# A Mamba-2 and FFN layer on one core: the Newton steps of the row factor and the sum of squares over column tiles move from VectorE to GpSimd

## The reference

```python
xn = _layernorm(x)
x = x + (xn + _mamba2(xn, w_in, conv_w, conv_b, dt_bias, A_log, D, norm_w, w_out)) + _ffn(xn, W1, W2, W3)
# _mamba2, with 16 heads of 64 (1024 inner columns) and a state of 128:
zxbcdt = xn @ w_in
xBC = silu(causal_conv4(zxbcdt[xBC columns]) + conv_b)
y = _ssd(xh * dt, dt * A, Bm, Cm) + xh * D
y = y * silu(z)
y = y * rsqrt(mean(y * y, axis=-1) + EPS) * norm_w      # the part that the change touches
return y @ w_out
# _ffn: silu(xn @ W1.T) * (xn @ W3.T), a Walsh-Hadamard transform over 2048 columns, @ W2.T
```

## Time and profile before

| | |
|---|---|
| median of 3 runs | 1002.5 us (1000.33 to 1004.55) |
| the profiled execution's own time | 1000.4 us |
| its span | 998.6 us |
| TensorE busy | 939.4 us (94%) |
| VectorE busy | 615.0 us (62%) |
| ScalarE busy | 352.1 us (35%) |
| GpSimd busy | 296.0 us (30%) |
| mean granted clock of TensorE | 0.982 |
| chain that ended last | TensorE 77%, VectorE 9%, issue 4%, ScalarE 4%, DMA 3%, GpSimd 3% |

### The profile page before, as it was taken

One profiled execution on the slowest core, in us unless ns is written; L12 is line 12 of the kernel. 1 busy time (PEld: TensorE's weight loads), 2 busy tenths in 40 slices (PEclk: granted clock), 3 DMA queues, 4 the chain that ended last, 5 costly groups with the idle time before them and its releaser, 6 DMA issues.

```text
span 998.6 us, 13195 instructions
## 1 busy us (share of the span) xinstructions
PE 939.4 (94%) x4960; PEld 469.5 (47%) x4960; DVE 615.0 (62%) x1063; ACT 352.1 (35%) x537; POOL 296.0 (30%) x180
## 2 busy tenths in 40 slices
PE   3797868999799999999999999999999999999997
PEld 2343333555344444555545445554545445555543
DVE  5776477779543576747762576766651766776721
ACT  5574744443423333331221343332221344232200
POOL 0332241636000021655500102654400202665300
PEclk9899997999899999999999999999999999999999
DMA  9589553746332433554421433554322535265122
GB/s 323 222 301 342 169 180 112 226 140 220 111 121 95 161 101 109 181 138 112 120 85 64 161 106 129 146 151 132 108 65 64 176 102 154 78 149 148 43 76 94
DMA packets 80815, 142.64 MB, mean 143 GB/s; under 512 B 8048, under 2 KB 20976, under 8 KB 78704
## 3 DMA queue, kind: packets, MB, share of 16 engines
q1 hardware_dynamic: 61536, 113.79, 35.7%
q10 hardware_dynamic: 19216, 28.01, 9.6%
HBM read 115.82 MB, written 25.95 MB: 142 GB/s over the span
## 4 chain that ended last, share of the span: by engine, by line
PE 77%; DVE 9%; issue 4%; ACT 4%; DMA 3%; POOL 3%; ACTq 0%; SPq 0%; DVEq 0%; POOLq 0%
PE ps L569 50%; PE ps L774 16%; PE ps L739 2%; PE ps L731 2%; DMA arena<-cs_rows 1%; DVE arena L1113 1%; PE ps L725 1%; PE ps L694 1%; DVE arena L1162 1%; PE ps L711 1%; ACT arena L862 1%; ACT arena L835 1%; POOL arena L1355 1%; DVE arena L1183 1%; POOL arena L1343 1%
## 5 line engine op out<-in xcount | busy, mean ns | idle before, releaser
L569 PE MATMUL ps<-xh,arena 128*128 128x512 f16 x1600 | 499.7, 386 | 28.4 <-DVE arena L1178 8.7
L569 PE MATMUL ps<-xl,arena 128*128 128x512 f16 x800 | 308.4, 385 | 0.0
L569 PEld LDWEIGHTS ps<-xh,arena 128*128 128x128 f16 x1600 | 160.4, 100 | 223.5 <-DVE arena L1113 25.8
L774 PE MATMUL ps<-arena 128*128 128x512 f16 x768 | 171.2, 379 | 0.0
L1328 POOL TENSOR_TENSOR arena<-arena 128x512 f16<-128x512 f32 x64 | 81.7, 1281 | 277.8 <-ACT arena L914 277.8
L1343 POOL TENSOR_TENSOR arena<-arena 128x2048 f32<-128x2048 f32 x16 | 57.8, 3612 | 286.6 <-DMA arena<-cs_rows 286.6
L569 PEld LDWEIGHTS ps<-xl,arena 128*128 128x128 f16 x800 | 79.2, 99 | 91.3 <-issue 7.3
L1162 DVE SCALAR_TENSOR_TENSOR arena<-ps,cw,arena 128x511 f32<-128x511 f32 (+2 forms) x120 | 89.5, 748 | 47.1 <-ACT arena L904 45.2
L774 PEld LDWEIGHTS ps<-arena 128*128 128x128 f16 x768 | 74.5, 98 | 91.2 <-issue 5.7
L914 ACT ACTIVATE arena<-arena 128x512 f16<-128x512 f32 x64 | 40.3, 630 | 207.6 <-DVE arena L1183 207.6
L569 PE MATMUL ps<-wo_hi,arena 128*128 128x512 f16 x256 | 78.8, 379 | 0.6 <-DVE arena L1291 0.6
(11 more groups left out here) (158 smaller groups left out, 1070.6 us busy)
## 6 DMA issues: line engine op xcount, KB each, us to landing
arena<-w_parts SPq DMA_DIRECT2D x198, 256.0 KB, 2.7
w_parts<-arena SPq DMA_DIRECT2D x66, 256.0 KB, 3.1
arena<-cs_rows ACTq DMA_DIRECT2D x16, 1024.0 KB, 6.0
arena<-w SPq DMA_DIRECT2D x8, 1024.0 KB, 8.6
arena<-w SPq DMA_DIRECT2D x32, 256.0 KB, 4.1
arena<-ecs_rows ACTq DMA_DIRECT2D x24, 256.0 KB, 7.9
arena<-w SPq DMA_DIRECT2D x8, 512.0 KB, 6.5
w_mid<-arena SPq DMA_DIRECT2D x16, 256.0 KB, 2.8
```

The lines of the kernel that those rows point to most:

```text
L569: ins = nc.tensor.matmul(out_ap, lhs(i, a), rhs(i, c), start=(i == 0 and s == 0), stop=(i == n - 1 and s == 2))
L774: ins = nc.tensor.matmul(bank(t), hw[a][:, i, t * P:(t + 1) * P], w2s[i % W2R][:, d, :], start=(i == 0 and s == 0), stop=(i == JF - 1 and ...
```

## The change

- The sum over column tiles (Q) is GpSimd's: three additions in place on `t1` (512, 256 and 128 columns wide, the last one into sqr), each waiting for the one before it.
- The three Newton steps are GpSimd's, as a new step ROW of 12 instructions of 128x1, which stands one FFN tile behind V. VectorE still makes the seed, and a column nmh = -0.5 * nv.
- The row factor moves from V to W on VectorE, and waits there for the root.
- V waits on TensorE also for yscl_ok; VectorE's t1 product waits for the sum of the chunk before.
- Four semaphores of the weight norms become one that counts to four (not shown: only names and numbers of the waits differ).

```diff
 STEP_FIRST = {"T": (3, 8, 17, 26), "E": (None, 7, 14, 22), "X": (4, 11, 18, 29), "Y": (7, 14, 22, 32), "N": (9, 16, 24, 34), "Q": (9, 16, 24, 34),
-              "V": (11, 18, 26, 36), "W": (14, 20, 28, 38)}
+              "V": (11, 18, 26, 36), "ROW": (12, 19, 27, 37), "W": (14, 20, 28, 38)}
 PREP_FIRST = {"LN": 28}
...
     "V": (10, 18, 26, 36),
+    "ROW": (11, 19, 27, 37),
     "W": (12, 20, 28, 38),
...
         Bs, Gm = view(P), view(P)
-        sqr, small = view(P), view(8)
-        ssum, ytot, yhalf, yscl, yinv, nv, nr, ntmp = (small[:, i:i + 1] for i in range(8))
+        sqr, small = view(P), view(9)
+        ssum, ytot, yhalf, yscl, yinv, nv, nr, ntmp, nmh = (small[:, i:i + 1] for i in range(9))
         row = view(1)
...
         mamba_evac = signal("mamba_evac", NC, 1)
+        guess_ok = signal("guess_ok", NC)
+        root_ok = signal("root_ok", NC)
         ln_ok = signal("ln_ok", 1)
...
                     elif kind == "V":
+                        pe.wait_ge(yscl_ok.sem, yscl_ok.at(b, c))
                         pe.wait_ge(sqr_ok.sem, sqr_ok.at(b, c))
...
                             dve.wait_ge(d_ecsb, (b * (NC - 1) + c) * 32)
+                            dve.wait_ge(sqr_ok.sem, sqr_ok.at(b, c - 1))
                             nc.vector.tensor_tensor(t1, bank(6, 2), ecsb, ALU.mult).then_inc(t1_ok.sem, 1)
...
                                                        op0=ALU.mult, op1=ALU.mult).then_inc(ygate_ok.sem, 1)
-                    elif kind == "Q":
-                        dve.wait_ge(sq_ok.sem, sq_ok.at(b, c))
-                        nc.vector.tensor_reduce(out=sqr, in_=t1.rearrange("p (q l) -> p l q", q=QE), axis=AX.X,
-                                                op=ALU.add).then_inc(sqr_ok.sem, 1)
                     elif kind == "N":
...
                         dve.wait_ge(mean_read.sem, mean_read.at(b, c))
-                        rsqrt(dve, steps, nv, nr, ntmp, yhalf)
-                        k = steps.step(nc.vector.tensor_scalar(row, nr, yinv, f_out[:, 0:1], ALU.mult, ALU.mult))
+                        k = steps.step(nc.vector.tensor_scalar(ntmp.bitcast(I32), nv.bitcast(I32), 1, None, ALU.logical_shift_right))
+                        steps.step(nc.vector.tensor_scalar(nmh, nv, -0.5, None, ALU.mult))
+                        dve.wait_ge(steps.sem, k)
+                        nc.vector.tensor_scalar(nr.bitcast(I32), ntmp.bitcast(I32), -1, 0x5F3759DF, ALU.mult,
+                                                ALU.add).then_inc(guess_ok.sem, 1)
                     elif kind == "W":
...
                                                                ALU.mult, ALU.add))
+                        dve.wait_ge(root_ok.sem, root_ok.at(b, c))
+                        k = steps.step(nc.vector.tensor_scalar(row, nr, yinv, f_out[:, 0:1], ALU.mult, ALU.mult))
                         dve.wait_ge(steps.sem, k)
...
         def _(pool):
+            newton = Steps(pool_steps)
             for b in range(NB):
...
                                                     ALU.mult).then_inc(xdec_ok.sem, 1)
+                    elif kind == "Q":
+                        pool.wait_ge(sq_ok.sem, sq_ok.at(b, c))
+                        k = newton.step(nc.gpsimd.tensor_tensor(t1[:, 0:4 * P], t1[:, 0:4 * P], t1[:, 4 * P:8 * P], ALU.add))
+                        pool.wait_ge(newton.sem, k)
+                        k = newton.step(nc.gpsimd.tensor_tensor(t1[:, 0:2 * P], t1[:, 0:2 * P], t1[:, 2 * P:4 * P], ALU.add))
+                        pool.wait_ge(newton.sem, k)
+                        nc.gpsimd.tensor_tensor(sqr, t1[:, 0:P], t1[:, P:2 * P], ALU.add).then_inc(sqr_ok.sem, 1)
+                    elif kind == "ROW":
+                        pool.wait_ge(guess_ok.sem, guess_ok.at(b, c))
+                        for n in range(3):
+                            k = newton.step(nc.gpsimd.tensor_tensor(ntmp, nr, nr, ALU.mult))
+                            pool.wait_ge(newton.sem, k)
+                            k = newton.step(nc.gpsimd.tensor_tensor(ntmp, ntmp, nmh, ALU.mult))
+                            pool.wait_ge(newton.sem, k)
+                            k = newton.step(nc.gpsimd.tensor_scalar(ntmp, ntmp, 1.5, None, ALU.add))
+                            pool.wait_ge(newton.sem, k)
+                            ins = nc.gpsimd.tensor_tensor(nr, ntmp, nr, ALU.mult)
+                            if n < 2:
+                                k = newton.step(ins)
+                                pool.wait_ge(newton.sem, k)
+                        ins.then_inc(root_ok.sem, 1)
                     elif kind == "S" and c > 0:
...
```

More of the change, by code:

```diff
@@ L234, in build @@
             sb(n, [P, 1]) for n in ("f_in", "f_half0", "f_half", "f_13", "f_out", "f_w2", "f_had"))
-        arena_words = 45669
+        arena_words = 45670
         arena = sb("arena", [P, arena_words])
@@ L344, in build @@
         guards = sem("guards")
-        sum_g0, sum_g1, sum_w2, sum_wo = sem("sum_g0"), sem("sum_g1"), sem("sum_w2"), sem("sum_wo")
+        norm_sums = sem("norm_sums")
         scale_g0, scale_g1, scale_13, scale_w2, scale_wo = (
@@ L418, in build @@
         ecst_ok = signal("ecst_ok", 1)
-        dve_steps, act_steps = sem("dve_steps"), sem("act_steps")
+        dve_steps, act_steps, pool_steps = sem("dve_steps"), sem("act_steps"), sem("pool_steps")
         N_PAR = 6
@@ L620, in _ @@
             pe.wait_ge(sq_g0, 3)
-            pe_norm(pe, SQ_G0, SQ_G0 + 4, sum_g0)
+            pe_norm(pe, SQ_G0, SQ_G0 + 4, norm_sums)
             pe_transposes(pe, 0, (2, 3))
@@ L660, in _ @@
                         pe.wait_ge(sq_g1, len(G1_PIECES))
-                        pe_norm(pe, SQ_G1, SQ_G1 + 5, sum_g1)
+                        pe_norm(pe, SQ_G1, SQ_G1 + 5, norm_sums)
                     elif kind == "K":
@@ L686, in _ @@
                         nc.tensor.matmul(bank(4)[:, 0:JF // 2 + 1], ones, row_sq[:, SQ_W2:SQ_W2 + JF // 2 + 1], start=True,
-                                         stop=True).then_inc(sum_w2, 1)
+                                         stop=True).then_inc(norm_sums, 1)
                     elif kind == "H":
@@ L697, in _ @@
                         pe.wait_ge(sq_wo, QE)
-                        pe_norm(pe, SQ_WO, SQ_WO + 9, sum_wo)
+                        pe_norm(pe, SQ_WO, SQ_WO + 9, norm_sums)
                     elif kind == "T":
@@ L1104, in _ @@
                                         ALU.add).then_inc(xn_dve, 1)
-            dve.wait_ge(sum_g0, 1)
+            dve.wait_ge(norm_sums, 1)
             to_scale(IN0, bank(FREE_BANK)[:, 0:4], ALU.add)
@@ L1198, in _ @@
                     elif kind == "G1S":
-                        dve.wait_ge(sum_g1, 1)
+                        dve.wait_ge(norm_sums, 2)
                         to_scale(IN1, bank(FREE_BANK)[:, 0:5], ALU.add)
@@ L1216, in _ @@
                     elif kind == "W2S":
-                        dve.wait_ge(sum_w2, 1)
+                        dve.wait_ge(norm_sums, 4)
                         to_scale(W2, bank(4)[:, 0:JF // 2 + 1], ALU.add)
@@ L1229, in _ @@
                     elif kind == "WOS":
-                        dve.wait_ge(sum_wo, 1)
+                        dve.wait_ge(norm_sums, 3)
                         to_scale(WO, bank(FREE_BANK)[:, 0:9], ALU.add)
```

## The result

The changed kernel takes 1071.1 us (median of four runs, 1061.5 to 1078.2) against 1002.6 us for the kernel before on the same chip: a ratio of 1.066, 95% interval 1.062 to 1.070. The ratio leaves out runs that are over 1.5% above the fastest of the same kernel (here the one of 1078.2 us, in e2 one of 1074.4). The changed kernel is slower by 68 us; forecast were 1054 us, 51 above before, and a range from 1026 to 1078. The profiled execution took 1072.4 us, 1070.6 of them the span.

What follows compares the result with a forecast made beforehand. The prediction took TensorE's gapless matmul stream in batches 1 to 3 as the bound. Its terms were 1000.4 us + 45 of stalls + 17.6 of clock - 8 in batch 0 = 1055, stated as 1054, range 1026 to 1078.

Steps and rivals of the forecast that it cites:

- What bounds the kernel: In batches 1 to 3 TensorE runs a gapless matmul stream; taking 65 us off VectorE is worth 0 there.
- The place in GpSimd's queue: GpSimd reaches the sum behind E, T and a low half, so TensorE stalls at V; chunk 3 does not.
- The size of the waits: Stalls of TensorE at V in batches 1 to 3, nine of 2 to 7 us each, 45 us together.
- The clock: After the stalls in batches 1 to 3 TensorE's granted clock falls, costing 17.6 us, bounds 0 and 28.
- Batch 0: Relieving VectorE closes TensorE's waits there, gaining about 8 us; a chunk 2 stall of some 4 us costs 0.
- the wait of 4.1 us at 168.5: Sign in batch 0: TensorE's longest wait, for VectorE's U5 eviction, would be gone in the changed profile.
- chunk 1, which was to have some 2 us to spare: In batch 0, chunk 1's sum on GpSimd would be hidden, done some 2 us before TensorE needs it at V.
- Newton off the path: Newton's 12 GpSimd instructions take 3.2 us, up to 4.5, hidden behind 24 output-projection matmuls before W needs the root.
- D: Rival: Newton steps also delay VectorE's evictions behind W, 9 to 27 us more, 1064 to 1080 us; chance 0.05.
- The sum: Forecast total for the profiled run: 1000.4 + 45 of stalls + 17.6 of clock - 8 of batch 0 = 1055 us.
- B: Rival: the sum is ready before V, leaving only batch 0's gain, 992 us, faster; chance 0.04.
- C: Rival: stalls at V without clock loss and with cheaper additions, 38 us of stall, 1030 us; chance 0.07.

Runs made afterwards that it cites:

- e2: Changed kernel with the Newton steps and row product back on VectorE, the column-tile sum still on GpSimd; 1065.6 us, ratio 1.059.
- e1: Changed kernel with the column-tile sum back on VectorE, the Newton steps still on GpSimd; 993.2 us, ratio 0.992.
- e3: Changed kernel with each chunk's sum ahead of the next chunk's E in GpSimd's queue, chunk 3 keeping its place; 995.7 us, ratio 0.994.
- e5: The changed kernel run once more, unaltered, as reference on another chip; 1072.6 us, ratio 1.073.
- e7: Changed kernel with VectorE's 128x2048 product of chunk 2 moved behind the seed of chunk 1 in batches 1 to 3; 1068.8 us, ratio 1.068.
- e6: Changed kernel with 48 unused matmuls on TensorE ahead of each wait at V, chunks 0 to 2 of batches 1 to 3; 1058.1 us, ratio 1.058.
- e9: Changed kernel with only the third addition of the sum left, covering two of eight column tiles; 1031.7 us, ratio 1.030.
- e4: Changed kernel with the change in batch 0 only, batches 1 to 3 running the code of before; 1002.2 us, ratio 1.001.

## Why the prediction was right, and where it wasn't

- **What bounds the kernel: right.** From 334 us on TensorE had no gap, so 65 us of relief for VectorE (measured 70.7) bought nothing there. The part after batch 0's last V takes 717.0 us in e1 and 715.8 in e3, as in the kernel before (715.5), with very different loads on VectorE (576.0, 546.3 and 615.0 us over the span).
- **The place in GpSimd's queue: right,** shown by e3, which only swaps the order of the sum and E. The waits come in nine chunks, none in chunk 3, as forecast.
- **The size of the waits: 45 forecast, 53.2 measured.** Chunk 0 of the three batches was forecast at 5.7 and 6.7 us in two of them and has 5.99 and 7.84; the additions took 2.59 us in batch 2 (660.76 to 663.35), with V at 663.50, against the 2.35 that were to cover both. Chunk 1 is where the working was too low: 2.1 us for batch 2, and 6.44 came. The trace divides it: 1.9 us for the third addition, shut out in all three batches and not in half of two; 2.2 us for E's DMA, which landed 7.8 us after its issue (685.74 to 693.53) and not 5.6 as before (654.41 to 659.98). The rest is 0.2 us of the additions. Not all chunks were forecast too low: chunk 2 of batch 2 was put at 4.1 us and has 3.09.

  Over the nine chunks of the changed kernel this DMA takes 4.4 to 8.7 us, and nearly all that differs between the batches is this DMA. E starts when it lands, and from there to V it is 14.2 us in chunk 0, 11.5 in chunk 1 and 10.5 to 10.6 in chunk 2, in all three batches. In chunk 2 the load took 8.6, 5.5 and 8.7 us, and the waits are 6.29, 3.09 and 6.42; in chunk 0 it took 4.4, 5.3 and 7.2, and the waits are 5.04, 5.99 and 7.84. The kernel before has nearly the same spread (4.9 to 7.9 us), and TensorE waited 0.6 us for GpSimd in all.

  The Trainium skill, SBUF — State Buffer, "Who interferes with whom", has it that the ports are an exclusive lock that one instruction keeps. The changed kernel agrees with it in the third addition of chunk 1 (2.38 us against 0.45 in three of three), e5 in the second (2.65 against 0.72, three of three), and e7 in the second of batch 1 (1.76). By that rule the prediction would have had 2 us more, as it said, and the rule was the better guide.

  The Trainium skill, Perfetto Trace Analysis, "Optimizing Scalar/DVE Operations", warns that moving work between VectorE and GpSimd might not help, because they share a port. Here that is the small part of the 68 us: in the nine chunks the additions were held by 5.8 us in chunk 1, 1.0 in batch 1's chunk 0 and 0.9 in batch 2's chunk 2, 7.6 in all, and e3 keeps the sum on GpSimd and is faster than before.
- **The clock: 17.6 forecast, 18.3 measured, 24.7 in e5.** It was sized from three stretches of batch 0, and the nine stretches after the waits cost 17.0 us by their own clocks, 1.9 us each. That forecast and first profile agree to 1 us is in part luck, as the same kernel lost 2.7 us a wait in e5. e6 shows that it is the clock: with the wait filled it is 1.00, and no time is left unexplained.
- **Batch 0: 8 us of gain forecast, 1.3 measured, and in e5 a loss of 1.1. This step failed.** The gain itself is there (8.1 us in e1, 9.2 in e3). What failed is the sentence "In chunk 2 a stall of some 4 us appears, but TensorE waits afterwards for the W2 factor anyway ...: 0". It takes the factor's time as fixed. If it were, the stall would cost nothing, but all that is gained ahead of it would be lost too, so a stall of 0 and a gain of 8 can't both hold. The matmul that waits for the factor, in the kernel before, the changed one and e1:

```profile
256.26 2.07 PE L694 MATMUL ps<-arena,hads 128*128 128x512 f32 x2 [4.99 <-DVE f_had L1219]
```

```profile
257.98 2.07 PE L697 MATMUL ps<-arena,hads 128*128 128x512 f32 x2 [2.43 <-DVE f_had L1223]
```

```profile
250.31 2.07 PE L697 MATMUL ps<-arena,hads 128*128 128x512 f32 x2 [3.87 <-DVE f_had L1223]
```

  From the mark that is 155.1 us before, 155.0 in the changed kernel and 147.5 in e1 (147.1 in e3, 147.9 in e9). VectorE makes the factor in order behind the evictions of TensorE's tiles, so a stall of TensorE delays it, and without the stall it comes earlier than before. Of the 7.5 us between the changed kernel and e1, 5.1 are the stall; 1.7 stand ahead of it (TensorE is ready for V 126.6 us after the mark, in e1 124.9) and 0.7 behind it, where the clock is 0.84 over 20 us and the wait for the factor 2.4 us against 3.9. The 1.3 us that are left came behind the factor, where the granted clock over 10 us is 0.83 in the changed kernel and 0.69 in the one before. e4 has the same stall alone and comes out at no change; e9 shortens it to 1.96 us and has 7 us back. Two smaller signs missed as well: the wait of 4.1 us at 168.5 is not gone, it fell to 1.8, and chunk 1, which was to have some 2 us to spare, had 0.5 and waits 1.9 us in e5.
- **Newton off the path: right.** Twelve steps take 3.3 us (664.70 to 667.97), as forecast at 3.2. e1 bears it out, and D is excluded. Between e2 and the changed kernel there are 5 us in e2's favour, about the size of the difference in their waits (49.1 and 53.8). The Newton steps didn't make these waits through the queue: in all nine chunks they are done before GpSimd waits for E's DMA, for 2.7 to 7.0 us, and none stands between E and the sum. Another way, at a size of 5 us, isn't excluded.
- **The sum.** 1000.4 + 53.2 + 18.3 - 1.3 = 1070.6, plus the 1.8 us by which the mark is later = 1072.4, the profiled time. Against the forecast of 1055 the misses are 8 us of wait, 7 of batch 0 and 1 of clock, all of one sign. They add up to 16 of the 72 us by which the profiled run is slower. The waits (53.2) lie above the 50 that the range allowed; the time stayed inside because the upper bound took 28 us for the clock.
- **The rivals.** B went by the busy shares (GpSimd was 30% busy). It is what e3 does, with a margin of 5 us that the place alone gives; in the order of the changed kernel it had no chance. C (no clock loss) is out: TensorE keeps its clock in e6, where it is kept busy, and not in the changed kernel. (Its 38 us of stall should have been 40, 45 less 5; that changes nothing.) That the loss is VectorE's delay is out as well: from 355 us on the changed kernel has no wait of TensorE for VectorE.
